# A selective-scan and gated-FFN block on one core: the last chunk's end as a program of its own, and weight casts in front of the first dt

## The reference

```python
xz = jnp.einsum('btd,pd->btp', x, W_xproj)          # 64 + 16 + 16 rows
dt_raw, Bm, Cm = xz[..., :64], xz[..., 64:80], xz[..., 80:]
dt = softplus(einsum('btr,dr->btd', dt_raw, W_dt) + b_dt)
dA = exp(dt[..., None] * -exp(A_log))
dBx = dt[..., None] * Bm[:, :, None, :] * x[..., None]
# over time: h = dA_t * h + dBx_t ;  y = sum over states of h * C_t
x = layernorm(x + ys + Dp * x)
gate, up = x @ (w_gate / 127).T, x @ (w_up / 127).T
x = layernorm(x + (silu(gate) * up) @ (w_down / 127).T)
```

## Time and profile before

| | value |
|---|---|
| median of 3 runs (range) | 2039.73 us (2038.73 to 2041.39) |
| the profiled execution | 2036.85 us |
| its span, first to last instruction | 2035.1 us |
| DVE busy | 1874.8 us (92%) |
| POOL busy | 1770.1 us (87%) |
| PE busy / weight loads | 1723.9 us (85%) / 1333.4 us (66%) |
| ACT busy | 1475.1 us (72%) |
| mean granted TensorE clock | 0.948 |
| DMA | 223.18 MB, mean 110 GB/s |

### The profile page before, as it was taken

How to read it: one execution, slowest core, us unless ns; L and a number is a source line. 1 busy time by engine, 2 the same in 40 slices (tenths; PEclk the granted TensorE clock), 3 DMA queues, 4 the chain that set the end, 5 groups by cost and what they waited for, 6 DMA issues and landing times.

```text
span 2035.1 us, 35587 instructions
## 1 busy us (share of the span) xinstructions
PE 1723.9 (85%) x10664; PEld 1333.4 (66%) x10664; DVE 1874.8 (92%) x2315; ACT 1475.1 (72%) x2668; POOL 1770.1 (87%) x809
## 2 busy tenths in 40 slices
PE   4688988888888988888988988988888988888885
PEld 2566776666667666676666776766677666677662
DVE  5999999999999999999999999999999999999973
ACT  5867777677877777777777877777877777877642
POOL 5998888999889998889998888998898898898950
PEclk7999999999999999999999999999999999999997
DMA  6324333234333333323333323333333333332200
GB/s 222 116 100 135 121 99 115 97 118 128 124 99 111 117 99 127 123 96 115 115 103 125 125 98 111 118 100 125 129 102 102 117 101 125 122 109 93 73 11 21
DMA packets 102675, 223.18 MB, mean 110 GB/s; under 512 B 9617, under 2 KB 44018, under 8 KB 102642
## 3 DMA queue, kind: packets, MB, share of 16 engines
q1 hardware_dynamic: 102642, 222.78, 33.1%
HBM read 203.87 MB, written 18.87 MB: 109 GB/s over the span
## 4 chain that ended last, share of the span: by engine, by line
PE 49%; issue 15%; ACT 14%; DVE 14%; POOL 6%; DVEq 1%; ACTq 0%; POOLq 0%; SPq 0%; DMA 0%
PE p_o L909 16%; PE p_y L872 13%; PE p_m L896 7%; POOL h L411 4%; DVE h L670 4%; DVE h L662 3%; DVE hid L706 3%; ACT p_da L514 3%; PE p_c L849 3%; PE p_m L820 3%; PE p_m L812 3%; ACT da_k L514 3%; ACT res_n L556 2%; PE p_da L840 2%; DVE silu_g L700 2%
## 5 line engine op out<-in xcount | busy, mean ns | idle before, releaser
L401 POOL TENSOR_TENSOR ub<-u,b_bc 128x1024 f32<-128x1024 f32 x384 | 905.8, 2373 | 0.1
L411 POOL TENSOR_TENSOR h<-h,c_bc 128x1024 f32<-128x1024 f32 x320 | 755.2, 2371 | 0.0
L514 ACT ACTIVATE p_da<-dt,neg_a 128x512 f32<-128x512 f32 x768 | 524.4, 686 | 231.7 <-DVE h L662 229.6
L872 PE MATMUL p_y<-ident,h 128*128 128x128 f32 x4096 | 562.3, 288 | 38.5 <-POOL h L411 38.4
L872 PEld LDWEIGHTS p_y<-ident,h 128*128 128x128 f32 x4096 | 506.4, 150 | 87.7 <-POOL h L411 52.7
L662 DVE TENSOR_TENSOR_SCAN h<-p_da,h_carry,ub 128x512 f32<-128x512 f32 x384 | 474.6, 1266 | 8.8 <-ACT p_da L514 8.0
L662 DVE TENSOR_TENSOR_SCAN h<-p_da,ub 128x512 f32<-128x512 f32 x384 | 452.4, 1208 | 9.8 <-ACT p_da L514 9.1
L909 PE MATMUL p_o<-wt_down,hid 128*128 128x256 f32 x1536 | 352.2, 379 | 2.2 <-DVE hid L706 1.4
L909 PEld LDWEIGHTS p_o<-wt_down,hid 128*128 128x128 f32 x1536 | 284.4, 190 | 51.0 <-issue 14.7
L896 PE MATMUL p_m<-x_t,wt_up 128*128 128x512 f16 x768 | 201.7, 385 | 80.8 <-DVE hid L706 80.8
L418 POOL TENSOR_TENSOR rstd<-var_eps,neg_half 128x8 f32<-128x8 f32 x33 | 54.0, 1636 | 235.0 <-DVE neg_mean L690 235.0
(11 more groups left out here) (76 smaller groups left out, 1850.2 us busy)
## 6 DMA issues: line engine op xcount, KB each, us to landing
b_bc<-bc_rows_dram SPq DMA_DIRECT2D x128, 768.0 KB, 4.0
c_bc<-bc_rows_dram SPq DMA_DIRECT2D x320, 256.0 KB, 4.3
x_in<-in_L_attn_x SPq DMA_DIRECT2D x32, 512.0 KB, 3.5
out_x<-res_n SPq DMA_DIRECT2D x32, 512.0 KB, 3.1
bc_rows_dram<-bc_rows SPq DMA_DIRECT2D x32, 64.0 KB, 1.6
hid<-in_L_ffn_w_gate SPq DMA_DIRECT2D x1, 768.0 KB, 4.9
hid<-in_L_ffn_w_up SPq DMA_DIRECT2D x1, 768.0 KB, 6.7
res<-in_L_ffn_w_down SPq DMA_DIRECT2D x1, 384.0 KB, 7.1
```

What stands on the lines that cost most here:

```text
L401: nc.gpsimd.tensor_tensor(ub[:, i % UB_SLOTS, :, :], u[:, par, :, :], b_bc[:, i:i + 1, :].broadcast_to([P, DH, T]), ALU.mult).then_inc(s_u ...
L411: nc.gpsimd.tensor_tensor(h[:, s % H_SLOTS, :, :], h[:, s % H_SLOTS, :, :], c_bc[:, i:i + 1, :].broadcast_to([P, DH, T]), ALU.mult).then_i ...
L514: nc.scalar.activation(da, dt[:, par, q, :], ACT.Exp, scale=neg_a[:, q, s:s + 1]).then_inc(s_da, 1)
L872: ins = nc.tensor.matmul(p_y_tok[:, k, q * P:(q + 1) * P], h[:, s % H_SLOTS, q, k * P:(k + 1) * P], ident[:, :], start=False, stop=(s == S ...
```

## The change

**The end.** `over_chunks` calls `tail(CHUNKS - 1)` in place of steps 32 and 33. In the tail: all remaining state sums of chunk 31 are issued before the down projection of chunk 30; the first norm of chunk 31 has its own inputs and scalars on 128x4 tiles and no longer waits for the second norm of chunk 30; `norm1` writes to `x_in`, so it waits for no residual; and the hidden tiles alternate between `p_m` and `p_da` (four PSUM banks), so the matmuls of tile j wait for silu and hidden of tile j-2.

**The start.** x is transposed before the projection weights, and PE waits for x alone there, then for `w_xproj` and `w_dt` (`s_proj_in`); ACT's exponential of `a_raw`, with its wait for the other four small loads, is issued behind the three first copies. On DVE, `weights_to_float()` stands before `dt_of(0, 0)`.

```diff
-            step(CHUNKS, 0, CHUNKS // 2, False, False, True, True)
-            step(CHUNKS + 1, 1, CHUNKS // 2, False, False, False, True)
+            tail(CHUNKS - 1)
...
-        SMALL_LOADS = 6
+        SMALL_LOADS = 4
@@ POOL
+            def norm_scalars_of(call, k):
+                pool.wait_ge(s_ln_in, 2 * call)
+                nc.gpsimd.tensor_tensor(rstd[:, k, :], var_eps[:, k, :], neg_half[:, k, :],
+                                        ALU.pow).then_inc(s_rstd, 1)
+                pool.wait_ge(s_rstd, call)
+                nc.gpsimd.tensor_tensor(shift[:, k, :], neg_mean[:, k, :], rstd[:, k, :],
+                                        ALU.mult).then_inc(s_ln, 1)
...
+            def tail(c):
+                norm_scalars_of(c + 1, 0)
+                norm_scalars_of(c + 2, 1)
+                pool.wait_ge(s_out_ready, c + 1)
+                norm_scalars_of(c + 3, 1)
@@ ACT
-            act.wait_ge(s_small_in, 16 * SMALL_LOADS)
-            nc.scalar.activation(neg_a[:, :, :], a_raw[:, :, :], ACT.Exp).then_inc(s_a_exp, 1)
+            act.wait_ge(s_xt_ps, 1)
+            nc.scalar.copy(x_t[:, 0, :, :], p_m[:, :, :]).then_inc(s_xt, 1)
...
-            x_out(0, 0)
+            act.wait_ge(s_small_in, 16 * SMALL_LOADS)
+            nc.scalar.activation(neg_a[:, :, :], a_raw[:, :, :], ACT.Exp).then_inc(s_a_exp, 1)
...
+            def tail(c):
+                z_out(c)
+                norm1(c, x_in)
+                x1_high(c)
+                for j in range(NH):
+                    tail_tanh(c, j)
+                norm2(c - 1, c + 2)
+                norm2(c, c + 3)
@@ DVE
+            weights_to_float()
             dt_of(0, 0)
-            weights_to_float()
...
+            def tail(c):
+                if N - 1 in DVE_STATES:
+                    times_c(c, N - 1, 1, CHUNKS // 2 - 1)
+                dve.wait_ge(s_z, c + 1)
+                norm_stats(0, z)
+                dve.wait_ge(s_stats[0], TT * (c + 1))
+                norm_mean(0)
+                norm_inputs_of(c + 1, 0, c + 1)
+                residual(c - 1, 0)
+                x1_low(c)
+                residual(c - 1, 1)
+                dve.wait_ge(s_res, 2 * c)
+                norm_stats(1, res)
+                dve.wait_ge(s_stats[1], TT * c)
+                norm_mean(1)
+                norm_inputs_of(c + 2, 1, c)
+                for j in range(NH):
+                    tail_silu(c, j)
+                    tail_hidden(c, j)
+                for a in range(2):
+                    residual(c, a, x_in)
...
@@ PE
             pe.wait_ge(s_const, 1)
-            pe.wait_ge(s_small_in, 16 * SMALL_LOADS)
+            pe.wait_ge(s_x_in, 16)
...
+            pe.wait_ge(s_proj_in, 16 * 2)
...
+            def tail_gate_up(c, j):
+                pe.wait_ge(s_x1_lo, c + 1)
+                for a, w, free, done in ((0, wt_gate, s_silu, s_gate_ps), (1, wt_up, s_hid, s_up_ps)):
+                    if j >= 2:
+                        pe.wait_ge(free, NH * c + (j - 1))
...
+            def tail(c):
+                if N - 1 in DVE_STATES:
+                    broadcast_c(c, N - 1, 1)
+                for s in range(max(SUM_LAG.values())):
+                    for lag in sorted(SUM_LAG.values(), reverse=True):
+                        if s < lag and SUM_LAG[s - lag + N in POOL_STATES] == lag:
+                            sum_states(c, s - lag + N, 1)
+                for i in range(6):
+                    down(c - 1, i // 2, i % 2, CHUNKS)
+                x1_transposed(c, False, True, x_in)
+                for i in range(6, 8):
+                    down(c - 1, i // 2, i % 2, CHUNKS)
+                for j in range(NH):
+                    tail_gate_up(c, j)
+                for i in range(8):
+                    down(c, i // 2, i % 2, CHUNKS)
```

More of the change, by code:

```diff
@@ L263, in sums, with over_chunks @@
             return N * c + (SUM_ORDER.index(s) + 1)
-        def over_chunks(eng, step):
+        def over_chunks(eng, step, tail):
             step(0, 0, 0, True, True, False, False)
@@ L289, in tiles @@
                 if sixth % 6 * zones // 6 == zone:
+                    assert slot < N
                     if slot == s and prev:
                         yield c - 1, j
-                    elif slot == s + N and last:
-                        yield c - 2, j
-        SMALL_LOADS = 6
+        SMALL_LOADS = 4
         WEIGHT_BATCHES = 2 * DH + 2
@@ L374, in step @@
                     broadcast_c(c + 1, 2, 1 - par)
-            over_chunks(sp, step)
+            def tail(c):
+                store(c - 1)
+                store(c)
+            over_chunks(sp, step, tail)
             sp.wait_ge(s_out, 16 * (CHUNKS + 1))
@@ L533, in z_out, with norm1 @@
                 nc.scalar.copy(z[:, :, :], p_y_tok).then_inc(s_z, 1)
-            def norm1(c):
+            def norm1(c, x1=x1):
                 act.wait_ge(s_ln, c + 1)
-                wait(act, s_res, 2 * c)
+                if x1 is not x_in:
+                    wait(act, s_res, 2 * c)
                 for k in range(TT):
@@ L549, in tanh_of, with norm2 @@
                                      scale=0.5 / (QUANT * X1_SCALE)).then_inc(s_tanh, 1)
-            def norm2(c):
-                act.wait_ge(s_ln, c + 2)
+            def norm2(c, call):
+                act.wait_ge(s_ln, call)
                 act.wait_ge(s_res, 2 * (c + 1))
@@ L610, in step @@
                         if last and due("norm2"):
-                            norm2(c - 2)
+                            norm2(c - 2, c)
                         if nxt and not prev and zone == 0 and s - AT["weights"][0] - 1 in range(WEIGHT_BATCHES):
@@ L617, in step, with tail_tanh @@
                             carry(c, s)
-            over_chunks(act, step)
+            def tail_tanh(c, j):
+                act.wait_ge(s_gate_ps, NH * c + (j + 1))
+                if j >= 2:
+                    act.wait_ge(s_silu, NH * c + (j - 1))
+                nc.scalar.activation(tail_t[j % 2], tail_ps[j % 2][:, 0, :], ACT.Tanh,
+                                     scale=0.5 / (QUANT * X1_SCALE)).then_inc(s_tanh, 1)
+            def tail(c):
[6 more added lines that the diff above has]
+                norm2(c, c + 3)
+            over_chunks(act, step, tail)
         @block.vector
@@ L708, in hidden, with residual @@
                                                silu_g[:, :], ALU.mult, ALU.mult).then_inc(s_hid, 1)
-            def residual(c, a):
+            def residual(c, a, x1=x1):
                 dve.wait_ge(s_o_ps, TT * c + 2 * (a + 1))
@@ L769, in _ @@
             pe.wait_ge(s_const, 1)
-            pe.wait_ge(s_small_in, 16 * SMALL_LOADS)
+            pe.wait_ge(s_x_in, 16)
+            for q in range(DH):
+                for k in range(TT):
+                    ins = nc.tensor.transpose(p_m[:, q, k * P:(k + 1) * P], x_in[:, k, q * P:(q + 1) * P], ident[:, :])
+            ins.then_inc(s_xt_ps, 1)
+            pe.wait_ge(s_proj_in, 16 * 2)
             for q in range(DH):
@@ L876, in sum_states, with x1_transposed @@
                 ins.then_inc(s_y, 1)
-            def x1_transposed(c, nxt, last):
+            def x1_transposed(c, nxt, last, x1=x1):
                 pe.wait_ge(s_x1, TT * (c + 1))
@@ L912, in down @@
                     ins.then_inc(s_o_ps, 1)
-            x_transposed(0)
             pe.wait_ge(s_wt, 2)
@@ L917, in _ @@
             pe.wait_ge(s_ones, 3)
+            pe.wait_ge(s_small_in, 16 * SMALL_LOADS)
             project_dt(0)
@@ L961, in step, with tail @@
                                 sum_states(cy, sy, py)
-            over_chunks(pe, step)
+            def tail_gate_up(c, j):
+                pe.wait_ge(s_x1_lo, c + 1)
+                for a, w, free, done in ((0, wt_gate, s_silu, s_gate_ps), (1, wt_up, s_hid, s_up_ps)):
+                    if j >= 2:
+                        pe.wait_ge(free, NH * c + (j - 1))
+                    for n in range(2 * DH):
+                        ins = nc.tensor.matmul(tail_ps[j % 2][:, a, :], w[:, n % DH, j * P:(j + 1) * P],
+                                               x1_t[:, n // DH, n % DH, :],
+                                               start=(n == 0), stop=(n == 2 * DH - 1))
+                    ins.then_inc(done, 1)
+            def tail(c):
+                if N - 1 in DVE_STATES:
[13 more added lines that the diff above has]
+                    down(c, i // 2, i % 2, CHUNKS)
+            over_chunks(pe, step, tail)
 _INS = ['L0_attn_x', 'L0_attn_W_xproj', 'L0_attn_W_dt', 'L0_attn_b_dt', 'L0_attn_A_log', 'L0_attn_Dp',
```

32 lines of the change are left out of this document (28 added, 4 removed).

## The result

The changed kernel takes 2023.65 us, the median of six runs from 2022.38 to 2025.21; the kernel before, run beside it, 2039.69 (2038.73 to 2041.39). The ratio is 0.9922, with a 95% interval from 0.9911 to 0.9933: 16.0 us by the medians. The profiled executions are 2022.87 and 2036.85 us, their spans 2021.1 and 2035.1: 14.0 us. The forecast was 2021.0, with a range from 2016 to 2027.

The account below looks back on a forecast made before the run. It took POOL to bound the start, DVE the loop and one dependency chain the end. End 15.3 us plus start 3.3 gave 18.6 us off, forecast 2021.0 us, range 2016 to 2027.

Parts of the forecast that it names:

- The end, items 1 to 6: Tail chain from state sums through first norm, gates and hidden tiles: last chunk's down projection starts 14.6 us earlier.
- from 1971 on: Tail: TensorE never idle over 0.9 us from 1971 us, so its clock was taken at the full level.
- item 6: Tail's six hidden tiles: DVE stays later than TensorE, 0.79 us a step, 1.58 a tile; down starts at 1998.5 us.
- The power on 128x4: Tail's last norm: power on 128x4 instead of 128x8 elements takes 0.9 us, saving 0.7.
- The start, items 1 to 4: Kernel start: projection 1.5 us earlier, short casts before dt, POOL instructions 1.8 us shorter, scans earlier; 3.3 us together.
- moves everything up to there: Start: POOL has no idle time from 22.62 to 106.16 us, so its earlier start or shorter instructions shift that whole stretch.
- rival C: Chunk loop gets slower as TensorE's clock dips fall where DVE waits; 0.62 us a chunk cancels the gain; chance 0.05.
- The ends I gave for the start: Bounds on the start's 3.3 us gain: 0 with late, dearer casts, 5 if TensorE's clock rises during the projection.
- Rival A, casts that hold dt: Start: casts slow by themselves end at 22.5 us and delay dt by 1.2 us; total 2024 us; chance 0.10.
- item 3: Start: POOL's `u_of` and five products return to undisturbed size without casts beside them, 1.8 us; nothing if DMA slows casts.
- Rival B, the lower clock in the tiles: Tail: TensorE stays at the lower clock in the hidden tiles, 3.44 us a tile; total 2030 us; chance 0.07.
- Rival D, only the end counts: First chunk bound by DVE, ACT and PE in turn, leaving 1.5 us of the start; 2023 us; shares chance 0.78.

Follow-up runs that it names:

- early fillers: Kernel with fillers in all stages, its early unused transposes moved in front of TensorE's waits in step 1: 1973.94 us with the new start, 1978.51 with the old.
- the norms were tied: Kernel with fillers in all stages, the tail's two norms tied again and all eight down halves before turning x1: 1990.41 us.
- fillers in the loop: Changed kernel plus 16 unused identity transposes per loop chunk, in TensorE's idle time before x1 is turned: 1981.53 us.
- the later start: Changed kernel plus two unused products on POOL between the first dt and the first u: 2026.68 us.
- the reworked end: Kernel with early fillers, second norm's statistics of chunk 30 behind the hidden tiles, late down halves in free banks, last residual per token tile: 1972.61 us.
- fillers in all stages: Kernel with fillers in the loop, plus unused transposes in the first two steps, the last step and the tail's head: 1980.58 us, 1979.82 with the old start.

## Why the prediction was right or wrong

- **The end, items 1 to 6: right.** The forecast was, from the last product by C: z at 2.6, x1 turned at 11.3, gate at 14.8, down at 27.3 us. With only the end changed, the trace has 2.62, 11.24, 14.71 and 26.94. In the profiled execution of the full change z came 1.4 us later, since the three sums ran at the lower clock; the step that took the full level "from 1971 on" was 3.0 us too early. With only the end changed the tail gained 15.6 us, 0.3 over the forecast's 15.3; the slow sums took 1.4 of them, and 14.2 are left. The steps of DVE in the tiles are 0.76 us apart on the mean, not 0.79, and TensorE's 1.72 us a tile set the last of them, where item 6 had DVE as the later one throughout.
- **The power on 128x4: mis-sized by a little.** It takes 1.01 us against 1.64; 0.63 us saved where I took 0.7.
- **The start, items 1 to 4: right in place, wrong in worth.** Projection, casts, POOL's start and sizes all came out, and POOL was 3.6 us ahead at 102 us. The step that failed is the sentence that whatever moves POOL's start "moves everything up to there", with the earlier one that POOL is the bound because it is never idle. POOL was busy all along, yet at 106 us it already waited 0.48 us for a chain that ran through TensorE, and with the earlier start TensorE spent more of the stretch from 80 to 106 us at the lower clock: 13.6 us in the changed kernel and 10.2 with only the start changed, against 3.4 in the kernel before and with only the end changed. The kernel pair with early fillers shows it: with the clock held, the 3.2 us arrive.
- **The profile of before had the sign.** Its window from 98.0 to 102.1 us has a granted clock of 0.58, and the product by C behind it waited 1.78 us for TensorE, in front of POOL's first wait (timeline of DVE, kernel before):

```profile
104.70 1.22 DVE L670 TENSOR_TENSOR h<-h,p_c 128x1024 f32<-128x1024 f32 x1 [1.78 <-PE p_c L849]
```

  In the forecast I read the timelines of POOL and DVE up to 106 us and the clock only as a mean; I costed the two levels for the tail and, in rival C, for the loop as a danger, never as what held the loop's time.
- **The ends I gave for the start were 0 and 5,** and the result lies near 0. The forecast's total was 2.7 us low, inside the range, because the range had this end, and partly by luck: by the two profiled executions the gain is 14.0 us of the 18.6, and 16.0 only by the medians. The 2.0 us between them are the scatter of single executions: those of before are spread over 2036.75 to 2041.71 us.
- **Rival A, casts that hold dt: out.** Two casts of 1536 elements take 1.83 us together and one of 768 takes 0.55, as against 3.10 and 2.70 beside POOL; POOL's u goes from 2.98 to 2.34. The casts now run at another time, with other DMA traffic, so their own times don't separate the two views of item 3. POOL's six instructions do: they take 13.9 in place of 15.8 us, from 21 us on as before, with 372 GB/s moved from 20 to 30 us (342 before). This agrees with the exclusive lock on the shared ports that the Trainium skill describes ("SBUF — State Buffer", section "SBUF: two separate sides").
- **Rival B, the lower clock in the tiles: out for this change,** but seen when the norms were tied (14.56 us from gate to down in place of 12.24).
- **Rival C: wrong way round.** The loop didn't get slower. It had been slow all the time.
- **Rival D, only the end counts: the nearest number, 2023, with another mechanism.** It kept 1.5 us of the start because the first chunk would be bound by other engines. The first chunk went as forecast, POOL was 3.4 to 3.6 us ahead up to 102 us, and what then held it was the clock. It shared the forecast's 0.78, so the chances did not tell the two apart.

What stays open: why the clock falls at one idle time of TensorE and not at another of nearly the same length. In the loop idle times of 2.2 to 2.4 us are followed by a fall. At TensorE's wait for a scan near 87 to 92 us, an idle time of 2.58 us was followed by a fall within 1 us of its end with only the start changed and with fillers in the loop. In the kernel before the same idle time was followed by 8 us at the full level, and one of 3.15 us with the later start by another 8 us. So the length of the idle time alone does not decide it, and no run here shows what does. Open too is how much of a late start of 4.7 us reaches the end: 3.0 us by the median, 1.1 at the last dt of the trace. The profiled execution of that kernel is the shortest of its five (2023.25 us) and had no slow sums in the tail.

## What to carry to other kernels

An engine that is never idle up to some time bounds the work only if no other engine would be late soon after; look at what it waits for at its first idle time, and at how late that one is. Where TensorE isn't the bound but stands in the chain, read its granted clock per stretch and not as a mean: idle time of 2 to 3 us per iteration was paid with 3 to 7 us at half speed behind it, and cheap unused transposes in that idle time, in a bank that is free there, took 42 us off a kernel of 2024. They helped in front of the wait; behind it, in the first chunks, the clock had already fallen when they began. An end that is written out on its own is worth reading as one chain, and its parts are to be tested in place, since they share slack.

## What the runs showed that I had not expected

- Sixteen unused transposes a chunk (1.97 us at the full level) shorten each chunk by 1.40 us, and the whole kernel from 2023.65 to 1981.53 us. With the early fillers and the reworked end it is 1972.61, 3.3% under the kernel before.
- The new start has two outcomes. The first dt comes at 19.7 to 20.0 us in five profiled executions and at 21.5 to 21.6 in five others (the old start: 21.3 to 21.4 in all four). In the late ones the second projection runs at the lower level, here that of the kernel with fillers in all stages, 3.75 us; in the early ones it takes about 2:

```profile
13.25 3.75 PE L912 MATMUL p_m<-rank_t,wt_dt 65*128 65x512 f32 x4 [1.36 <-ACT bc_rows L497]
```

  So of the 1.5 us that the earlier projection brings, all is lost in half of the executions. I had the clock in the start only as a gain, in the upper end of the range.
- For the first 15 to 17 us the profile gives a granted clock of 1.00, though the first projection's 3.65 us are twice what the same four matmuls take later at the full level (1.88 us). I go by the durations there.
